# A vision tower in one kernel: the maximum rows' DMAs issued from ScalarE, and five side stages at other tiles

## The reference

```python
h = tok(x, W)
h = h + attn0(layernorm(h), ...)
h = h + ffn0(layernorm(h), ...)
h = h + attn1(layernorm(h), ...)
h = h + ffn1(layernorm(h), ...)
```

## Time and profile before

| | us |
|---|---|
| median of 3 runs | 4682.24 |
| lowest, highest | 4676.37, 4692.46 |
| the profiled execution's own time | 4679.61 |
| its span, first to last instruction | 4677.8 |
| TensorE busy | 4016.9 (86%) |
| VectorE busy | 2908.0 (62%) |
| ScalarE busy | 2733.2 (58%) |
| GpSimd busy | 858.5 (18%) |
| mean granted TensorE clock | 0.939 of full |

### The profile page before, as it was taken

One profiled execution on the slowest core, in us unless ns is written; L12 is line 12 of the kernel. 1 busy time (PEld: TensorE's weight loads), 2 busy tenths in 40 slices (PEclk: granted clock), 3 DMA queues, 4 the chain that ended last, 5 costly groups with the idle time before them and its releaser, 6 DMA issues.

```text
span 4677.8 us, 61163 instructions
## 1 busy us (share of the span) xinstructions
PE 4016.9 (86%) x21509; PEld 1329.1 (28%) x21509; DVE 2908.0 (62%) x4956; ACT 2733.2 (58%) x4896; POOL 858.5 (18%) x1263
## 2 busy tenths in 40 slices
PE   2487898998989988898998899899888989989877
PEld 1122322323232232323223232332223223222222
DVE  2365666757666675666767576675656667576652
ACT  0154575656656565665666566566656656666564
POOL 2111212112121210312211131221213122121210
PEclk9598999999999999999999999999999999999898
DMA  2221212201222221122212112221221122011100
GB/s 47 45 42 28 41 38 44 38 17 28 40 42 37 36 36 27 28 37 44 37 30 36 32 28 37 44 38 25 31 42 28 38 44 38 17 28 34 16 13 5
DMA packets 115603, 156.28 MB, mean 33 GB/s; under 512 B 21391, under 2 KB 63119, under 8 KB 115261
## 3 DMA queue, kind: packets, MB, share of 16 engines
q1 hardware_dynamic: 115297, 152.36, 18.5%
HBM read 120.01 MB, written 29.36 MB: 32 GB/s over the span
## 4 chain that ended last, share of the span: by engine, by line
PE 64%; DMA 12%; ACT 8%; DVE 7%; issue 4%; SPq 3%; POOL 1%; ACTq 0%; POOLq 0%; DVEq 0%
PE acc L843 17%; PE st L829 16%; PE nat L809 15%; DMA q_rows<-max_rows 7%; DVE tile_max L1230 5%; PE side L675 3%; PE side L778 3%; DMA x_rows<-in_x 2%; SPq L553 2%; DMA k_rows<-k_scratch 2%; ACT hidden L1000 2%; PE side L652 2%; ACT prob L1027 2%; PE side L764 2%; PE side L732 1%
## 5 line engine op out<-in xcount | busy, mean ns | idle before, releaser
L1230 DVE TENSOR_REDUCE tile_max<-nat 128x1 f32<-128x512 f32 x4096 | 2605.5, 685 | 1566.6 <-PE nat L809 1552.6
L1027 ACT ACTIVATE prob<-st 128x512 f32<-128x512 f32 x4096 | 2303.0, 597 | 1747.7 <-PE st L829 1699.0
L829 PE MATMUL st<-q_rows,k_rows 99*128 99x512 bf16 x4096 | 1595.0, 390 | 255.9 <-DMA q_rows<-max_rows 197.9
L809 PE MATMUL nat<-k_rows,q_rows 96*128 96x512 bf16 x4096 | 1462.9, 390 | 118.4 <-DMA k_rows<-k_scratch 89.6
L843 PE MATMUL acc<-prob,v_padded 128*32 128x512 f32 x8192 | 1118.7, 619 | 1.0 <-ACT prob L1027 1.0
L829 PEld LDWEIGHTS st<-q_rows,k_rows 99*128 99x128 bf16 x4096 | 399.6, 98 | 1552.1 <-ACT prob L1027 1040.4
L809 PEld LDWEIGHTS nat<-k_rows,q_rows 96*128 96x128 bf16 x4096 | 405.2, 99 | 663.1 <-DVE tile_max L1230 304.4
L1383 POOL TENSOR_SCALAR max_parts<-neg_max 128x16 bf16<-128x16 f32 x128 | 26.3, 206 | 1907.9 <-DVE neg_max L1237 1433.4
L843 PEld LDWEIGHTS acc<-prob,v_padded 128*32 128x32 f32 x8192 | 162.7, 109 | 351.2 <-issue 310.2
L1310 POOL TENSOR_SCALAR ln_s<-ln_s 128x8 f32<-128x8 f32 x64 | 13.0, 203 | 1157.7 <-DVE ln_s L1135 1157.7
L675 PE MATMUL side<-x_rows,w_patch 128*128 128x512 f32 x256 | 149.9, 740 | 83.5 <-DMA x_rows<-in_x 83.5
(11 more groups left out here) (127 smaller groups left out, 2117.7 us busy)
## 6 DMA issues: line engine op xcount, KB each, us to landing
q_rows<-q_scratch SPq DMA_DIRECT2D x288, 128.0 KB
k_rows<-k_scratch SPq DMA_DIRECT2D x96, 384.0 KB
x_rows<-in_x SPq DMA_DIRECT2D x64, 512.0 KB, 6.6
q_scratch<-hidden SPq DMA_DIRECT2D x32, 384.0 KB
k_scratch<-hidden SPq DMA_DIRECT2D x96, 128.0 KB
group_weights<-in_routed SPq DMA_DIRECT2D x64, 129.0 KB, 3.9
q_rows<-max_rows SPq DMA_DIRECT2D x512, 3.0 KB
out_h<-out_rows SPq DMA_DIRECT2D x16, 256.0 KB, 2.0
```

The costliest lines, as they stand in the source:

```text
L809: eng.matmul(NAT[place % len(NAT)][:, :], QA[u][0:K_NAT, h, c:c + P], KA[u][0:K_NAT, h, kh * 512:kh * 512 + 512], start=True, stop=True)\
L829: eng.matmul(ST[n % 2][:, :], KA[u][0:K_ALL, h, t * P:t * P + P], QA[u][0:K_ALL, h, half * 512:half * 512 + 512], start=True, stop=True)\
L1027: eng.activation(prob[:, n % TILES, :], ST[n % 2][:, :], ACT.Exp).then_inc(exp_done, 1)
L1230: eng.tensor_reduce(mx[:, q % 2, j // 8, j % 8 // 2, j % 2:j % 2 + 1], NAT[place % len(NAT)][:, :], AX.X, ALU.max).then_inc(nat_free, 1)
```

## The change

`max_dma` moves from SyncE's block to ScalarE's, with the same wait (`nat_free`, for DVE's copy into `max_rows`) and the same four DMAs. On ScalarE it stands at n % 32 = 25 (`TURN + 2`), in front of that slot's exp. The semaphore step that `alone` put behind the wait (a counter that nobody waits for) is dropped.

In the pairs, TOKA moves from slot 82 to 78 and the second LX from 87 to 83; OUT moves from 79 to 82; TOKB, TOKC, LN1, LN2, TR, QK, QV, VC and SCR of the new item move one slot back, RL two. The second LX now stands 14 slots ahead of TOKB instead of 9. The first phase's table is not touched. Line numbers of the changed kernel differ: L1027 there is the same exp as before, the DMAs L581, L584 and L595 are L570, L573 and L584, and `max_dma`'s L553 is L994.

```diff
--- before.py
+++ after.py
@@ -174,20 +174,20 @@
         put(48, "FW", r - 1)
         for k in range(E + 1):
             put(51 + 3 * k, f"FY{k}", r - 1)
-        put(79, "OUT", r - 1)
+        put(82, "OUT", r - 1)
     if f2:
-        put(82, "TOKA", r + 2)
-        put(87, "LX", r + 2, 1)
-        put(96, "TOKB", r + 2)
-        put(101, "TOKC", r + 2)
-        put(104, "LN1", r + 2, "0")
-        put(110, "LN2", r + 2, "0")
-        put(118, "TR", r + 2, "0")
-        put(121, "QK", r + 2, 0)
-        put(125, "QV", r + 2, 0)
-        put(130, "VC", r + 2, 0)
-        put(134, "SCR", r + 2, 0)
-        put(138, "RL", r + 2, 0)
+        put(78, "TOKA", r + 2)
+        put(83, "LX", r + 2, 1)
+        put(97, "TOKB", r + 2)
+        put(102, "TOKC", r + 2)
+        put(105, "LN1", r + 2, "0")
+        put(111, "LN2", r + 2, "0")
+        put(119, "TR", r + 2, "0")
+        put(122, "QK", r + 2, 0)
+        put(126, "QV", r + 2, 0)
+        put(131, "VC", r + 2, 0)
+        put(135, "SCR", r + 2, 0)
+        put(140, "RL", r + 2, 0)
         put(232, "HO0", r + 2)
     if f3:
         put(96, "WCL", r + 1)
@@ -542,17 +542,6 @@
                          PT[0:WINDOW, s, :].unsqueeze(1).to_broadcast([WINDOW, H, N_TOK]))
             N_SET_DMA.append(n_dma[0])
             eng.wait_ge(s_dma, n_dma[0])
-
-            def max_dma(kind, it, n0, q, last=False):
-
-                a, b, g, half = super_of(kind, it, q)
-                v0 = over(n0, SUPER)
-                turn = RING_USES * (v0 + q + 1) + (0 if last else TURN)
-                alone(eng.wait_ge(nat_free, at(turn + 1)))
-                for hh in range(HEADS):
-                    eng.dma_start(QA[buffer_of(a, b)][K_MAX:K_ALL, HEADS * g + hh, half * 512:half * 512 + 512],
-                                  mrow[4 * PARTS * hh:4 * PARTS * hh + 4 * PARTS, q % 2, :])\
-                        .then_inc(maxrow_in[q % 2], 16)
 
             def side_stage(stage, n):
                 name, b, _, _, *more = stage
@@ -600,14 +589,7 @@
                     for k, stage in enumerate(side):
                         side_stage(stage, found[0, k])
                     return
-                if kind == "first":
-                    max_dma(kind, it, n0, 0)
                 for n in range(n_tiles(kind)):
-                    ahead = n + SUPER + LEAD
-                    if ahead % SUPER == TURN:
-                        q = ahead // SUPER - 1
-                        if kind != "last" or q < SUPERS:
-                            max_dma(kind, it, n0, q, last=(kind == "last" and q == SUPERS - 1))
                     for k, stage in enumerate(side[n]):
                         side_stage(stage, found[n, k])
 
@@ -1002,6 +984,17 @@
                 eng.wait_ge(he_ready, at(2 * E * (b + 1)))
                 eng.sem_inc(xt_used, 1)
 
+            def max_dma(kind, it, n0, q, last=False):
+
+                a, b, g, half = super_of(kind, it, q)
+                v0 = over(n0, SUPER)
+                turn = RING_USES * (v0 + q + 1) + (0 if last else TURN)
+                eng.wait_ge(nat_free, at(turn + 1))
+                for hh in range(HEADS):
+                    eng.dma_start(QA[buffer_of(a, b)][K_MAX:K_ALL, HEADS * g + hh, half * 512:half * 512 + 512],
+                                  mrow[4 * PARTS * hh:4 * PARTS * hh + 4 * PARTS, q % 2, :])\
+                        .then_inc(maxrow_in[q % 2], 16)
+
             def acc_out(half, n0, q):
 
                 if q % SUPERS == 1:
@@ -1017,7 +1010,14 @@
                             hidden(stage[1], found[0, k], 0)
                         side_stage(stage, found[0, k])
                     return
+                if kind == "first":
+                    max_dma(kind, it, n0, 0)
                 for n in range(n_tiles(kind)):
+                    ahead = n + SUPER + LEAD
+                    if ahead % SUPER == TURN + 2:
+                        q = ahead // SUPER - 1
+                        if kind != "last" or q < SUPERS:
+                            max_dma(kind, it, n0, q, last=(kind == "last" and q == SUPERS - 1))
                     for k, stage in enumerate(side[n]):
                         if stage[0] == "FW":
                             hidden(stage[1], found[n, k], n)
```

## The result

The changed kernel takes **4756.16 us** (median of 4 runs, 4750.06 to 4774.73), the kernel before 4682.24 (median of the three runs in the table above; a fourth, at 12908.56 us, is left out, and its cause is not known). The ratio of the means is 1.0161 with a 95% interval of 1.012 to 1.0202: slower by 1.6%. The forecast was 4486, its range ended at 4620. The profiled execution took 4774.73, the slowest of the four, 18.6 above their median; its span is 4772.9.

A forecast was written before the change was run, and what follows sets the result against it. TensorE was taken as the bound, idle mostly in DMA waits. -280 (maximum rows) + 28 (sharing) - 94 (x) + 143 (ScalarE issues) + 7 (moved stages) = -196 on 4679.6, plus 2.6 to the median: 4486 us, range 4400 to 4620.

The forecast's parts named there:

- What bounds the kernel: TensorE, idle mostly in DMA waits: maximum rows queued behind an RL on SyncE (197.9 us), x (83.5 us), plus lost clock.
- Part 3: Four DMAs in ScalarE's list delay exp 25 and so `st` 27 by 1.3 us in quiet groups: +143 us.
- the list is read ahead of the work: On ScalarE, issues start once DVE's copy is there, while exps 23 and 24 run; reason for taking 1.3 us.
- beginning before exp 24 ends: Sign of being right: L994 on ScalarE takes 0.7 us and starts before exp 24 ends.
- TensorE gaps of this size leave its clock alone: At `st` 27, the 1.3 us gaps cost no clock, since after one gap of 1.64 us it read 1.00.
- the issue also costs clock, and it gets slower: Rival, 5%: issues start once exp 24 has ended, TensorE gaps of 2.4 us plus 1.7 us lost clock; 4777.
- the maximum rows still wait behind the RL: Rival, 6%: moving the DMAs to ScalarE doesn't free the maximum rows from the RL; +56, giving 4738.
- Part 1: Maximum rows leave SyncE's queue: their 197.9 us of waits and 82 us of lost clock go, -280; sharing costs +28.
- +28 us for sharing: Two loaded queues share the DMA engines: 1 us taken for each of the 28 maximum-row waits; bounds nothing to 280.
- Part 2: Second half of x issued earlier in the pairs: 14 waits of about 4.9 us go, -69, with clock -94.
- Part 4: Moved side stages: TOKA's copy and OUT's transposes share a PSUM bank, 14 x 0.5 = +7; nothing for RL, SCR, QK, QV.
- The signs on record: Right: two x waits, clock about 0.96, 0.7 us issues. Wrong: half clock at slot 28, waits at slots 32 and 160.

The follow-up runs named there:

- e5_rl_later: e1_moves_only with each pair's two RLs put behind the maximum rows in SyncE's list (slots 16 to 28, 140 to 156); 4351.65 us.
- e7_three_one: The changed kernel with three of the four maximum-row DMAs before exp 25 and the fourth before exp 28; 4594.24 us.
- e10_change_paced: The changed kernel with the RLs at slots 30 and 158 and SyncE waiting for `st` of that slot ahead of them; 4706.65 us.
- e3_spread: The changed kernel with one of the four maximum-row DMAs on ScalarE before each of exps 25 to 28; 4527.31 us.
- e2_scalar_only: The changed kernel with the old table of side stages, so only the maximum rows' issues move to ScalarE; 4742.62 us.
- e6_spread_rl: e3_spread with the two RLs at table slots 28 and 156; 4533.27 us.
- e11_rl_only: The kernel before with only the RLs moved, from slots 16 and 138 to 28 and 156; 4417.07 us.
- e1_moves_only: The kernel before with only the table's new slots for side stages, the maximum rows' DMAs staying on SyncE; 4624.12 us.

## Why the prediction was wrong

**What bounds the kernel: right.** The queue served in order, an RL ahead of the maximum rows twice in a pair, and clock lost behind each wait: e5_rl_later removes just that and the x waits, and gains 331 us, where the forecast's terms for it (-280, -94 and +7) give -367.

**Part 3 failed, and it decided the sign.** It was on record as +143 us; measured by itself it is 355. The 212 us that it lacked are most of the 270 between the forecast and the result; some 61 of them are gap (204 for 143), the rest is clock. Two steps of it were wrong:
- *The start of the issue.* I let it begin right behind DVE's copy while exps 23 and 24 still run, because "the list is read ahead of the work", for 1.3 us a group. It begins only once exp 24 has started, at 2325.83 against a copy that ended at 2325.31. That is the case that the text priced at 1.8, and 1.81 is what the gap is. The evidence for reading ahead was 0.03 us of overlap between back-to-back exps; it shows that an exp can start 0.03 us before the one ahead of it ends, not that an instruction can overtake a predecessor that still waits for its input. In this case no group's first DMA behind an exp that waits for `st` started before that exp did. The sign on record, "beginning before exp 24 ends", came true and said nothing: it fits 1.8 as well as 1.3. The issue's duration was right (0.70 taken, 0.73 measured). With 95 gaps of 1.8, 16 of 0.70 and 16 of 1.36 (slots 57 and 121; the trace has 96, 14 and 14) the idle time is 204 us, and the waits view's +206 agrees.
- *"TensorE gaps of this size leave its clock alone."* One window behind one gap of 1.64 us stood for this. Behind two thirds of the 1.8 us gaps (59 of 89) the clock falls for 3.4 us or more; behind e7_three_one's gaps of 1.1 us it stays (82 of 84). At 1.1 us the clock held, at 1.8 it did not, and the 1.3 us that I had assumed lies between, nearer to the first; so the second error hung at least in part on the first. It costs 163 us in e10_change_paced against e5_rl_later. Four at once instead of three (e7_three_one to the change) costs 162 us, most of it clock.

**The rival that came nearest in its mechanism** was "the issue also costs clock, and it gets slower", at 4777 with a chance of 5%. Its place and its turning point (a quiet group that loses over 3.1 us in all) are what happened: 1.8 of gap and 1.7 of clock, 3.3 on the mean. Only its gap of 2.4 was too long. It deserved much more than 5%: three possible starts of the issue had been named, with 1.3, 1.8 and 2.4, nothing measured chose between them, and two of the three led to where the clock had not been seen to be safe. The other slow rival, "the maximum rows still wait behind the RL" at 4738, was as near in number, by luck: it kept all of these waits, which fell to 54 us, and it had no clock lost behind the issues.

**Part 1: half right.** The maximum rows do pass an RL in part: behind the RL of slot 140 their first packet comes 7.8 us after the issue (median) instead of 14.1. Some of that is the RL's earlier start in the changed kernel; but in e3_spread, where the issue follows the RL's start by 12.5 us much as before (12.2), it is 7.6. In the changed kernel all 13 waits left are at slot 160; at slot 32 the RL now starts 22 us ahead of the issue instead of 17. But +28 us for sharing was far too little: the 1 us for each of the 28 waits was an estimate that no run shows, and the price is 138 where no pause covers it. The DMA view of the changed kernel, the first 7.4 us behind an issue at 1948.56, then the next 4, shows how it is shared:

```profile
DMA packets 312, 0.59 MB, mean 80 GB/s; under 512 B 24, under 2 KB 24, under 8 KB 312
q1 hardware_dynamic: 312, 0.59, 53.9%
...
DMA packets 180, 0.27 MB, mean 68 GB/s; under 512 B 50, under 2 KB 50, under 8 KB 180
q10 hardware_dynamic: 34, 0.01, 1.9%
```

For 7.4 us not one packet of q10 goes through, while q1 moves 312. I had read "the reader has some 6 us" off the distance between issue and use, and then set the landing at 3 us, the time that the packets took once they were served. The rival "the maximum rows still wait behind the RL" had part of the truth: the order on the shared engines wasn't turn by turn from the first packet on. What holds q10's packets back for those microseconds no run here shows; that stays open.

**Part 2: right in size, wrong in whose doing it was.** The x waits went (4.9 each). But the earlier trace rows already had SyncE at its maximum rows until 2120.06, 4.2 us behind `x_used`; part 1 took that away, and with it the wait. The forecast credited the term to the moves alone, though it had the row. In the changed kernel the moves bring nothing measurable (the change against e2_scalar_only: +14, and the intervals of the two ratios overlap).

**Part 4** had +7 for the moved stages, against 24 us of small waits. Of the RL's move it said "nothing for these"; with SyncE untied, the table's slot for the RL no longer sets its start (140 or 156 made no difference, e3_spread and e6_spread_rl), which the forecast did not see.

**The sum, in the runs' numbers:** -331 for both DMA waits gone (e5_rl_later), +355 for four issues at once on ScalarE, +50 for the RL that the new queue still meets: +74, and 4756.16 - 4682.24 is +74 too. That agreement proves nothing, since each term is the step from one run to the next. What supports the terms is what the traces show in each step: for the second, idle and clock rise by 358 together (195 and 163); for the third, they rise by 70 (48 and 22), and 53.9 us of waits for the maximum rows appear that e10_change_paced doesn't have.

**The signs on record.** The x waits went down to the opening's two and an issue took 0.73 us, as expected. But two of the signs of being wrong were there, half clock behind `st` 27 and waits for the maximum rows at slot 160 (13, up to 7.4 us; those at slot 32 were gone), and the mean clock stayed at 0.938, where about 0.96 was expected.

## What to carry to other kernels

A DMA issue costs the engine that makes it its place in the list (0.73 us each on ScalarE here), so ask what stands behind it and how long a gap that makes on the bound engine; four at once made one gap of 1.8 us here, one at a time next to none (55.5 us of waits for the exp in all, against 51.3 before). Before a small urgent transfer is given another queue, look at what lies ahead of it in its own: putting the bulk transfer behind it, where its reader has time, was worth 5.6% here, and the waits for what it loads did not grow (`nat` for `k_rows`: 86.5 us in e11_rl_only, 89.6 before). And when a wait leaves an engine's list, ask what else it had been pacing.

## What the runs showed that I had not expected

- In the changed kernel a DMA in ScalarE's list behind an exp that waits starts when that exp starts, with 0.01 us between the two rows, not when its own semaphore is there (0.5 us earlier).
- Half clock behind TensorE gaps depended steeply on the gap: 2 of 84 at 1.1 us, 59 of 89 at 1.8 us. Length isn't all. In the changed kernel 8 of 14 gaps of 1.1 us, all at slot 125, had it too, two slots behind a gap of 1.4 us at slot 123; in e1_moves_only the gaps of 1.1 us at slot 125 have no such gap ahead of them, and none of the 14 had it. Why 30 of the 89 gaps of 1.8 us did not have it stays open.
- A second queue under load was not served turn by turn from its first packet: 7.8 us to the first packet of 256 B behind the RL of slot 140, 1.4 us at the same place without one (e10_change_paced).
